# A gated attention block with a 32-expert layer: the gates are laid over the partitions by DMA, the output matrix is folded into the values, and all engines get new orders

## The chip, the cores and the metric

The kernel runs on one core of a Trainium2 chip. The metric is the device time of one execution in microseconds (us). Before the change it is 139.21 us, the median of three runs (139.1 to 139.27). The execution that the profiler recorded took 139.16 us; its span, from the first to the last recorded event, is 137.4 us, so 1.76 us lie around the span.

Engines are named as in the profile: PE is TensorE (PEld its weight loads), DVE is VectorE, ACT is ScalarE, POOL is GpSimd, SP is SyncE, which here only issues DMAs.

## The reference, cut to what matters

```python
# x (4, 256, 128), ctx (4, 256, 96), mask (4, 256) over ctx rows; 2 heads of 64; 32 experts of 64, top 4
xn = layernorm(ctx) * g + b;  ln = layernorm(layernorm(x)) * g + b
q  = ln @ Wq.T
kv = concat([xn @ Wkv.T, ln @ Wlkv.T], axis=1);  k, v = kv[..., :128], kv[..., 128:]
attn = softmax(where(mask, rmsnorm(q) * scale @ rmsnorm(k).T, -big))    # 256 queries x 512 keys, per head
x  = x + tanh(g_xattn) * ((attn @ v) @ Wo.T + bo)
xm = layernorm(x)
gates = sigmoid(xm @ expert_sel.T);  all but the 4 largest of 32 set to 0
h  = relu(einsum('nd,edf->nef', xm, keys)) * gates[:, :, None]
x  = x + tanh(g_ffn) * einsum('nef,efv->nv', h, values)
```

## The kernel before, in words

All data stays on the chip: 4 batches (b) of 256 rows, as 8 tiles of 128 rows. Each engine runs one list of stages, written out by hand in `PE_ORDER`, `DVE_ORDER` and `ACT_ORDER` (L56 to L99). A stage name stands in several lists, and semaphores tie its parts together. No scheduler moves anything: the list is the order.

Attention, per batch. `stats_in` and `norm_in` (DVE) normalize the rows, `turn_in` transposes them, and `project` (L746, L750) multiplies them by Wq and both key/value matrices in plain float32. ACT squares q and k and copies all of it from PSUM to `proj` (L603 to L611). `sum_qk` and `norm_qk` make the RMS norm, `turn_qk` transposes q and k and splits each into two float32r parts (`hi` and the rest `lo`), which PE multiplies faster than float32. `row_max` (PE L773, DVE L453) finds the largest score of each row, `turn_max` turns it into a row, and `weights b.i` (L801 to L807) computes scores minus maximum with the keys on the partitions, which ACT exponentiates into `prob` (L647). `attend b.a` (L818) multiplies by the values of head a, ACT copies the result to `oT` (L656), and `out_proj` (L828) applies Wo. DVE divides by the row sums and adds x (L468 to L478).

Expert layer. `stats_mid`, `norm_mid` and `turn_mid` make `xm`, transposed and split; `select` computes the gates on DVE; POOL cuts them into three bf16 parts (L342 to L345), and `turn_gates` transposes these. The expert columns are cut into 16 chunks of 128 (two experts each), the rows into two halves of 512. `up h.c` computes a chunk of hidden values in three float32r matmuls (L717 to L719) and spreads the gates of its two experts over the 128 partitions with a fourth matmul against a 0/1 matrix `expand` (L873). ACT applies the relu (L686), DVE multiplies by the spread gates (L542), ACT and DVE split the product into `hid_hi` and `hid_lo` (L693, L550), and `down h.c` adds three more matmuls into the accumulator of the half. `finish` turns the sum back with PE transposes (L892), and DVE adds the residual (L557).

Each engine waits in its own list: `up` on PE for the relu of two chunks before, `down` for both parts of its chunk. SP issues all input loads first (L277 to L286) and then waits for the results (L290).

## Time and profile before

| | |
|---|---|
| median of three runs | 139.21 us |
| profiled execution, its span | 139.16 us, 137.4 us |
| PE busy | 117.6 us, 86% |
| DVE busy | 108.7 us, 79% |
| ACT busy | 82.4 us, 60% |
| POOL busy | 18.6 us, 14% |
| largest DVE group (L542, gates times relu) | 32 x 689 ns |
| largest ACT groups (L693 split, L686 relu) | 32 x 628 ns, 32 x 596 ns |
| data moved by DMA | 4.28 MB, nearly all in the first 14 us |

Busy time of PE is the union of its records; the records of pipelined matmuls overlap, so the step from one start to the next is what a matmul costs in a row, and the mean duration is longer. A float32 matmul leaves two records, a float32r one leaves one. "Idle before" is the time that an engine stood still ahead of a group, with what ended it. Some matmul records are missing.

### The profile page before, as it was taken

What the parts mean: (1) busy time and instruction counts of PE and PEld (TensorE: products, weight loads), DVE (VectorE), ACT (ScalarE), POOL (GpSimd) and SP (SyncE); (2) the same over time, 40 slices, a digit from 0 to 9 for tenths busy, and PEclk for the clock granted to TensorE, in tenths of its full rate; (3) what the DMA queues carried; (4) which work ended last, traced back from release to release, by engine and by line L of the source; (5) the groups of instructions that cost most, each with busy time, mean ns of one, the idle gap of its engine ahead of it and who ended that gap; (6) DMA issues with size and microseconds to landing.
All of it is one profiled execution on the core that took longest, in us unless ns stands there. A gap on an engine that the chain in (4) does not pass through costs nothing.

```text
span 137.4 us, 2089 instructions
## 1 busy us (share of the span) xinstructions
PE 117.6 (86%) x616; PEld 81.3 (59%) x616; DVE 108.7 (79%) x333; ACT 82.4 (60%) x188; POOL 18.6 (14%) x43
## 2 busy tenths in 40 slices
PE   5917955696879799799896999999998999999990
PEld 5904534353646497378673676667766667767760
DVE  5877699887979959698496699998994799769852
ACT  5214698749893255337546756764575687587720
POOL 4050000700012493000330000004040000000000
PEclk9995599959999999999999999999999999999998
DMA  4699000000000000000000000000000000000004
GB/s 87 203 366 389 12 2 0 0 2 0 5 0 0 0 0 5 2 0 0 0 5 0 0 0 0 0 2 0 0 0 7 0 0 0 0 0 0 2 5 153
DMA packets 2171, 4.28 MB, mean 31 GB/s; under 512 B 240, under 2 KB 1648, under 8 KB 1904
## 3 DMA queue, kind: packets, MB, share of 16 engines
...
## 4 chain that ended last, share of the span: by engine, by line
PE 65%; DVE 18%; ACT 6%; issue 6%; POOL 1%; POOLq 1%; DVEq 0%; ACTq 0%
PE bank L717 10%; PE bank L719 9%; PE bank L718 9%; PE bank L818 9%; PE bank L873 5%; PE bank L746 4%; PE bank L750 3%; PE bank L828 3%; PE bank L773 3%; PE bank L801 2%; DVE keys L542 2%; PE bank L803 2%; PE bank L807 1%; PE bank L805 1%; DVE shift_l L365 1%
## 5 line engine op out<-in xcount | busy, mean ns | idle before, releaser
L542 DVE TENSOR_TENSOR keys<-bank,values 128x512 f32<-128x512 f32 x32 | 21.9, 689 | 7.6 <-ACT values L686 6.4
L686 ACT ACTIVATE values<-bank 128x512 f32<-128x512 f32 x32 | 19.1, 596 | 12.8 <-PE bank L719 12.8
L550 DVE TENSOR_TENSOR hid_lo<-keys,hid_hi 128x512 fp32r<-128x512 f32 x32 | 21.2, 683 | 0.8 <-ACT hid_hi L693 0.4
L693 ACT ACTIVATE hid_hi<-keys 128x512 fp32r<-128x512 f32 x32 | 19.6, 628 | 2.5 <-PE bank L719 1.6
L717 PE MATMUL bank<-hid_hi,v_lo 128*128 128x512 f32 x32 | 16.2, 506 | 0.0
L818 PE MATMUL bank<-prob,proj 128*65 128x256 f32 x64 | 15.1, 382 | 0.2 <-ACT prob L647 0.2
L717 PE MATMUL bank<-xm_hi,k_lo 128*128 128x512 f32 x32 | 14.6, 455 | 0.6 <-ACT gateT L677 0.6
L647 ACT ACTIVATE prob<-bank 128x512 f32<-128x512 f32 x16 | 8.9, 594 | 9.4 <-PE bank L807 7.8
L873 PE MATMUL bank<-gateT,expand 96*128 96x512 bf16 x32 | 12.5, 391 | 0.9 <-DVE keys L542 0.8
L719 PE MATMUL bank<-hid_hi,v_hi 128*128 128x512 f32 x32 | 12.7, 396 | 0.0
L718 PE MATMUL bank<-xm_lo,k_hi 128*128 128x512 f32 x32 | 12.6, 395 | 0.0
L718 PE MATMUL bank<-hid_lo,v_hi 128*128 128x512 f32 x32 | 12.6, 394 | 0.0
L719 PE MATMUL bank<-xm_hi,k_hi 128*128 128x512 f32 x32 | 12.6, 393 | 0.0
L453 DVE CUSTOM_DVE_ANT_0 junk<-bank,mask_b 128x512 bf16<-128x512 f32 x16 | 10.4, 689 | 2.5 <-PE bank L773 2.5
L818 PEld LDWEIGHTS bank<-prob,proj 128*65 128x65 f32 x64 | 8.4, 138 | 4.8 <-ACT prob L647 0.5
L746 PE MATMUL bank<-wa,xnT 128*128 128x384 f32 x16 | 8.8, 688 | 2.7 <-ACT xnT L591 2.7
L773 PE MATMUL bank<-kT_hi,qT_hi 64*128 64x512 f32 x16 | 6.3, 495 | 5.4 <-DVE mx L453 2.9
L325 POOL TENSOR_TENSOR k_lo<-keys,k_hi 128x512 fp32r<-128x512 f32 x4 | 5.0, 1269 | 32.5 <-ACT k_hi L621 32.5
L873 PEld LDWEIGHTS bank<-gateT,expand 96*128 96x128 bf16 x32 | 3.1, 96 | 10.5 <-DVE keys L542 5.8
L773 PEld LDWEIGHTS bank<-kT_hi,qT_hi 64*128 64x128 f32 x16 | 2.4, 183 | 9.2 <-DVE mx L453 5.9
L717 PEld LDWEIGHTS bank<-xm_hi,k_lo 128*128 128x128 f32 x32 | 6.1, 191 | 1.6 <-issue 0.7
L342 POOL CAST gate_p<-gate 128x64 bf16<-128x64 f32 x4 | 0.9, 237 | 44.4 <-DVE gate L531 44.4
...
## 6 DMA issues: line engine op xcount, KB each, us to landing
...
out<-x_mid SPq DMA_DIRECT2D x4, 128.0 KB, 1.9
...
cx<-ctx_in SPq DMA_DIRECT2D x2, 96.0 KB, 2.8
...
```

Source lines behind the costliest of these rows:

```text
L453: dve.tensor_tensor_reduce(junk[:, n % 2, :], bank_of(b, ROW_MAX + i)[:, :], mask_b[:, b, :], 1.0, SENTINEL, ALU.add, ALU.max, mx[:, b, i ...
L542: dve.tensor_tensor(hid[:, n % 3, :], gates_bank(n)[:, :], relu[:, n % 2, :], ALU.mult).then_inc(hid_ready, 1)
L550: dve.tensor_tensor(hid_lo[:, n % RING, :], hid[:, n % 3, :], hid_hi[:, n % RING, :].bitcast(F32), ALU.subtract).then_inc(hid_lo_ready, 1)
L686: act.activation(relu[:, n % 2, :], bank[H_BANK[n % 2]][:, :], ACT.Relu).then_inc(relu_ready, 1)
L693: act.activation(hid_hi[:, n % RING, :], hid[:, n % 3, :], ACT.Copy).then_inc(hid_hi_ready, 1)
L717: pe.matmul(o, ll, rh, start=start, stop=False)
L718: pe.matmul(o, lh, rl, start=False, stop=False)
L719: return pe.matmul(o, lh, rh, start=False, stop=stop)
L746: last = pe.matmul(bk[:, 0:G * DH], xnT[:, b, P * i:P * i + P], wa[:, A_LAT:A_LAT + G * DH], start=True, stop=True)
L773: pe.matmul(bank_of(b, ROW_MAX + i)[:, :], qT_hi[rows, b, P * t:P * t + P], kT_hi[rows, b, :], start=True, stop=True).then_inc(max_done, 1)
L818: last = pe.matmul(head_bank(b, a)[0:DH + 1, 0:S], proj[:, b, t, 4 + a, :], prob[:, a, t, :], start=(t == 0), stop=(t == KT - 1))
L873: pe.matmul(gates_bank(n)[:, :], expand[:, cc], half(gateT, h), start=True, stop=True).then_inc(spread_done, 1)
```

## The change

1. Gates. The `expand` matmul, POOL's three-part split and ACT's relu go. The gates are transposed in float32 (`turn_gates`), written by SP to a DRAM tensor `gate_rows`, and read back per chunk as a 128 x 512 tile `gated` (256 KB) in a ring of 6 slots: 64 copies outermost, the two experts inside. The columns of keys and values are interleaved to match. DVE's `up` takes relu and gate in one instruction, straight from PSUM.
2. The first 8 chunks of the first half (`WHOLE`) are not split; `down` multiplies them in plain float32, in one matmul each. The hidden banks become three.
3. Values. `fold` multiplies Wo into the value matrices once; `vlat` and `vctx` compute values that already carry Wo, one set of 128 columns per head. `project` keeps only q and k; `norm_qk` reads them from PSUM. `attend b.t` uses `prob` as the stationary side and gives rows by 129 columns, so `oT` and `out_proj` on PE go.
4. End. The output leaves transposed; `turn_res` transposes the residual ahead, and `finish` is one DVE instruction per batch.
5. Start. Most memsets leave DVE for POOL or become ACT copies; the 12 warm-up matmuls become 24 (`warm`), 16 of them ahead of `turn_in 0`. POOL makes the low parts of keys and values only behind the first matmul of each `row_max`.
6. All three order lists are new.

```diff
-WARM_UP = 12
+WARM_UP = 1
+WHOLE = 8
 # SP
-            sp.dma_start(wb[:, :], wb_in).then_inc(in_wb, 16)          # (now ahead of mask_in)
+            for h in range(HALF):
+                for b in range(HB * h, HB * h + HB):
+                    sp.wait_ge(gateT_ready, b + 1)
+                    sp.dma_start(gate_rows[:, S * b:S * b + S], gateT[:, b, :]).then_inc(rows_out[h], 16)
+                sp.wait_ge(rows_out[h], 16 * HB)
+                for c in range(EC):
+                    n = EC * h + c
...
+                    if n >= SLOTS:
+                        sp.wait_ge(hid_ready, n - SLOTS + 1)
+                    sp.dma_start(gated[:, n % SLOTS, :],
+                                 gate_rows[2 * c:2 * c + 2, HN * h:HN * (h + 1)].unsqueeze(0).to_broadcast([F, 2, HN])).then_inc(gated_in[n % SLOTS], 16)
 # DVE, up
-                dve.wait_ge(relu_ready, n + 1)
-                dve.wait_ge(spread_done, n + 1)
-                dve.tensor_tensor(hid[:, n % 3, :], gates_bank(n)[:, :], relu[:, n % 2, :], ALU.mult).then_inc(hid_ready, 1)
+                dve.wait_ge(up_done, n + 1)
+                dve.wait_ge(gated_in[n % SLOTS], 16 * (n // SLOTS + 1))
+                free_hid(n - 3)
+                dve.scalar_tensor_tensor(hid[:, n % 3, :], bank[H_BANK[n % len(H_BANK)]][:, :], 0.0, gated[:, n % SLOTS, :],
+                                         ALU.max, ALU.mult).then_inc(hid_ready, 1)
 # DVE, norm_qk
+                for lo, hi, src in ((0, KT * HEADS, bank_of(b, PROJECT)[:, :]), (KT * HEADS, NR, bank_of(b, PROJECT + 1)[:, 0:S])):
+                    dve.tensor_tensor(qk[:, b, lo:hi, :], src.rearrange("p (r d) -> p r d", d=DH),
...
 # ACT
+            def constants(i):
+                act.activation(ident_b[:, :], ident[:, :], ACT.Copy).then_inc(ident_b_ready, 1)
+                act.activation(mask_b[:, :, S:], ident[:, 0:1].unsqueeze(2).to_broadcast([P, B, S]), ACT.Copy,
+                               scale=0.0).then_inc(open_ready, 1)
+                act.activation(cnT[DC:DC + 1, :, :], ...
-                act.activation(relu[:, n % 2, :], bank[H_BANK[n % 2]][:, :], ACT.Relu).then_inc(relu_ready, 1)
-                act.activation(oT[:, b % 2, a, :], head_bank(b, a)[0:DH + 1, 0:S], ACT.Copy).then_inc(oT_ready, 1)
+                act.activation(vw[:, b, BT:, :, 0:D], value_bank(b, 0)[:, :]...   # vlat; vctx likewise
 # PE
+            def fold(i):
+                pe.wait_ge(wo_ready, 1)
+                for a in range(HEADS):
+                    pe.matmul(bank[7][:, D * a:D * a + D], wb[:, B_LV + D * a:B_LV + D * a + D], wo, start=True, stop=True)
...
+            def vlat(b):
+                        last = pe.matmul(o, lat, folded[:, D * a:D * a + D], start=True, stop=(a > 0))
+                        if a == 0:
+                            pe.matmul(o, wb[:, B_ONE:B_ONE + P], wb[:, B_WO:B_WO + D], start=False, stop=True)
+            def vctx(b):
+                    last = pe.matmul(bk[:, HEADS * D * t:HEADS * D * (t + 1)], cnT[:, b, P * t:P * t + P],
+                                     folded[0:DC + 1, HEADS * D:], start=True, stop=True)
-                    last = pe.matmul(head_bank(b, a)[0:DH + 1, 0:S], proj[:, b, t, 4 + a, :], prob[:, a, t, :],
+                        last = pe.matmul(bank_of(b, OUT + t)[:, WOA * a:WOA * a + WOA], prob[:, b % 2, a, j, P * t:P * t + P],
+                                         vw[:, b, j, a, :], start=(j == 0), stop=(j == KT - 1))
 # PE, down
+                if n < WHOLE:
+                    last = pe.matmul(bank[ACC_BANK[h]][:, :], values[:, cc], hid[:, n % 3, :],
+                                     start=(c == 0), stop=(c == EC - 1))
 # PE, up
-                pe.matmul(gates_bank(n)[:, :], expand[:, cc], half(gateT, h), start=True, stop=True).then_inc(spread_done, 1)
```

What the change moves shows at three places. First DVE's list from its start, before:

```order
L365 MEMSET shift_l 97x2048
L368 MEMSET shift_l 1x4x128 x2
L369 MEMSET mask_b 128x4x128
L370 MEMSET eps 128x1
L371 MEMSET shift_c 128x776
L373 MEMSET shift_c 128x8x2
L391 BN_STATS bn_in<-vecs_x 128x6 x2
```

and now:

```order
L360 MEMSET shift_l 97x2048
L379 BN_STATS bn_in<-vecs_x 128x6 [waits in_x0,dve_step]
L379 BN_STATS bn_in<-vecs_x 128x6
L382 BN_STATS bn_in<-cx 128x6 [waits in_cx0]
L382 BN_STATS bn_in<-cx 128x6
```

Five memsets and the small one behind them no longer stand ahead of the first statistics (`bn_in`). Second, PE's list where the attention ends and the expert layer begins (L855 turns gates, L818 attends, L717 to L719 and L873 are `up`, L836 turns `xm`, L828 is the output projection), before:

```order
L828 MATMUL bank<-wb,oT 128x129 x4
L855 MATMUL bank<-ident_b,gate_p 96x128 x2
L818 MATMUL bank<-prob,proj 65x256 x4
L855 MATMUL bank<-ident_b,gate_p 96x128 x2
L717 MATMUL bank<-xm_hi,k_lo 128x512
L718 MATMUL bank<-xm_lo,k_hi 128x512
L719 MATMUL bank<-xm_hi,k_hi 128x512
L873 MATMUL bank<-gateT,expand 128x512
```

and now (L879 turns gates, L854 attends, L705 to L707 are `up`, L862 turns `xm`):

```order
L879 MATMUL bank<-ident,gate 32x128 x2
L854 MATMUL bank<-vw,prob 128x129 x8
L879 MATMUL bank<-ident,gate 32x128 x2
L854 MATMUL bank<-vw,prob 128x129 x16
L705 MATMUL bank<-xm_hi,k_lo 128x512
L706 MATMUL bank<-xm_lo,k_hi 128x512
L707 MATMUL bank<-xm_hi,k_hi 128x512
L862 MATMUL bank<-ident,xn 128x128 x2
```

Both halves of the last batch's `attend` now stand between the second turned gates and the first chunk; before, one head of it and the last output projection followed inside the expert layer. Third, SP's queue behind the input loads, before:

```order
L286 DMA values<-values_in 128x2048
L290 DMA out<-x_mid 128x256 x4
```

and now (`inT` is the memory in which the ring `gated` lies):

```order
L288 DMA values<-values_in 128x2048
L292 DMA gate_rows<-gateT 32x256 [waits gateT_ready] x2
L302 DMA inT<-gate_rows 128x1x512 [waits vlat_done,vctx_done,proj_done,rows_out0]
L302 DMA inT<-gate_rows 128x1x512 x5
L302 DMA inT<-gate_rows 128x1x512 [waits hid_ready] x10
L292 DMA gate_rows<-gateT 32x256 [waits gateT_ready] x2
L302 DMA inT<-gate_rows 128x1x512 [waits hid_ready,rows_out1]
L302 DMA inT<-gate_rows 128x1x512 [waits hid_ready] x15
L306 DMA out<-x_mid0 128x256 [waits res_ready] x4
```

Four writes and 32 loads of 256 KB are added to a queue that had nothing to do there, and each load behind the sixth waits for DVE's product of six chunks before.

## Rows read from the trace of the kernel before

**Rows 1.** Four stretches of the span: busy us of each engine, clock, DMA.
```profile
0.00:35.25 35.25, 24.52 (x84) 16.15 (x85) 28.04 (x109) 21.18 (x62) 5.77 (x21) 0.85 0.30 103
35.25:72.92 37.67, 33.43 (x266) 23.67 (x265) 29.88 (x113) 20.82 (x47) 9.64 (x14) 1.00 0.01 2
72.92:132.48 59.56, 58.30 (x261) 40.70 (x261) 49.13 (x108) 39.77 (x78) 3.20 (x8) 1.00 0.00 1
132.48:137.40 4.92, 1.31 (x9) 0.76 (x7) 1.66 (x4) 0.66 (x2) 0.00 (x0) 0.88 0.34 110
```

**Rows 2.** Groups by shape: busy us, mean ns, idle before, releaser.
```profile
L542 DVE TENSOR_TENSOR keys<-bank,values 128x512 f32<-128x512 f32 x32 | 21.9, 689 | 7.6 <-ACT values L686 6.4 <-PE bank L873 0.6
L550 DVE TENSOR_TENSOR hid_lo<-keys,hid_hi 128x512 fp32r<-128x512 f32 x32 | 21.2, 683 | 0.8 <-ACT hid_hi L693 0.4 <-DVE keys L542 0.2 <-issue 0.2
L439 DVE SCALAR_TENSOR_TENSOR kT_lo<-bank,vecs_x,kT_hi 128x512 fp32r<-128x512 f32 x4 | 3.0, 738 | 0.5 <-ACT kT_hi L638 0.5
```

**Rows 3.** Timeline of PE, the last `down`: start, us, engine, line, operation.
```profile
132.02 0.39 PE L718 MATMUL bank<-hid_lo,v_hi 128*128 128x512 f32 x1
132.25 0.39 PE L719 MATMUL bank<-hid_hi,v_hi 128*128 128x512 f32 x1
```

**Rows 4.** Timeline of the front, DVE, ACT and PE, to the first row maximum.
```profile
1.24 1.76 DVE L365 MEMSET shift_l<- 97x2048 bf16 x1 [1.24 <-PEq L947]
2.94 0.20 ACT L583 ACTIVATE tanh_g<-vecs_x 128x2 f32<-128x2 f32 x1 [0.92 <-DMA vecs_x<-x_in]
...
6.02 0.28 DVE L391 BATCH_NORM_STATS2 bn_in<-vecs_x 128x6 f32<-128x128 f32 x1
...
11.11 0.56 ACT L591 ACTIVATE xnT<-bank,vecs_x 128x256 f32<-128x256 f32 x1 [3.33 <-PE bank L733]
...
16.89 0.95 DVE L423 TENSOR_REDUCE ss<-sq 128x12 f32<-128x768 f32 x1 [1.25 <-ACT sq L609]
...
24.40 0.80 PE L773 MATMUL bank<-kT_hi,qT_hi 64*128 64x512 f32 x2 [1.97 <-DVE kT_lo L439]
```

**Rows 5.** Stretches of the front by clock, same columns as Rows 1.
```profile
1.53:6.84 5.31, 5.31 (x24) 5.12 (x24) 4.61 (x14) 1.98 (x3) 0.68 (x8) 1.00 0.71 186
10.00:16.50 6.50, 5.75 (x14) 3.30 (x15) 4.75 (x30) 3.00 (x11) 0.21 (x1) 0.50 0.55 232
...
27.00:30.25 3.25, 3.25 (x7) 1.68 (x7) 3.11 (x12) 1.46 (x6) 0.00 (x0) 0.50 0.01 3
```

**Rows 6.** Timeline of PE: projection, attend and output projection at the full clock.
```profile
32.34 1.56 PE L746 MATMUL bank<-wa,xnT 128*128 128x384 f32 x4 [0.85 <-ACT xnT L591]
43.62 1.89 PE L818 MATMUL bank<-prob,proj 128*65 128x256 f32 x8
...
58.49 1.16 PE L828 MATMUL bank<-wb,oT 65*128 65x129 f32 x8
```

**Rows 7.** DMA: two stretches during the loads (columns as Rows 1).
```profile
3.75:5.00 1.25, 1.25 (x8) 1.25 (x7) 0.98 (x3) 0.69 (x1) 0.00 (x0) 1.00 0.90 331
5.00:6.50 1.50, 1.50 (x9) 1.50 (x9) 1.37 (x6) 0.00 (x0) 0.00 (x0) 1.00 0.47 108
```

**Rows 8.** DMA issues: KB each, us from issue to landing.
```profile
out<-x_mid SPq DMA_DIRECT2D x4, 128.0 KB, 1.9
cx<-ctx_in SPq DMA_DIRECT2D x2, 96.0 KB, 2.8
```

**Rows 9.** Timeline of PE: the first chunk of the expert layer.
```profile
72.92 0.47 PE L717 MATMUL bank<-xm_hi,k_lo 128*128 128x512 f32 x1 [0.56 <-ACT gateT L677]
```

**Rows 10.** Timeline of the end, PE, ACT, DVE, SP's queue.
```profile
132.48 1.35 PE L892 MATMUL bank<-ident,xn 128*128 128x128 f32 x8
132.68 0.66 ACT L699 ACTIVATE xn<-bank 128x256 f32<-128x256 f32 x2 [1.89 <-PE bank L719]
133.12 1.66 DVE L557 SCALAR_TENSOR_TENSOR x_mid<-bank,tanh_g,x_mid 128x256 f32<-128x256 f32 x4 [1.55 <-PE bank L892]
133.63 1.80 SPq L290 DMA_DIRECT2D out<-x_mid  x4
```

More of the change, by code:

```diff
@@ L41 @@
 HN = HT * P
-G = 6
+SLOTS = 6
 NR = KT * HEADS + BT * HEADS
@@ L56 @@
 PE_ORDER = """
-    turn_in 0, project 0, turn_in 1, project 1, turn_in 2, turn_qk 0, row_max 0, project 2, turn_max 0,
-    turn_in 3, project 3, weights 0.0, turn_qk 1, weights 0.1, turn_qk 2, row_max 1, attend 0.0, turn_max 1,
-    attend 0.1, row_max 2, weights 1.0, turn_qk 3, out_proj 0, turn_max 2, weights 1.1, weights 2.0, attend 1.0,
-    attend 1.1, row_max 3, out_proj 1, weights 2.1, turn_max 3, turn_mid 0, attend 2.0, select 0, weights 3.0,
-    turn_mid 1, attend 2.1, select 1, weights 3.1, out_proj 2, turn_gates 0, attend 3.0, turn_gates 1, up 0.0,
@@ new lines @@
+    row_max 0, vlat 2, vctx 2, turn_max 0, project 2, turn_in 3, weights 0.0, vlat 3, turn_qk 1, vctx 3,
+    project 3, turn_qk 2, weights 0.1, row_max 1, attend 0.0, turn_max 1, attend 0.1, weights 1.0, row_max 2,
+    weights 1.1, turn_qk 3, turn_max 2, attend 1.0, row_max 3, attend 1.1, turn_max 3, weights 2.0, turn_mid 0,
+    weights 2.1, weights 3.0, turn_mid 1, select 0, attend 2.0, select 1, weights 3.1, turn_gates 0, attend 2.1,
+    turn_gates 1, attend 3.0, attend 3.1, up 0.0, turn_mid 2, up 0.1, select 2, up 0.2, up 0.3, down 0.0, up 0.4,
@@ L69 @@
+    turn_res 2, up 1.13, up 1.14, up 1.15, down 1.9, down 1.10, down 1.11, down 1.12, down 1.13, down 1.14,
+    down 1.15, turn_res 3
 """
 DVE_ORDER = """
[L71 to L74 removed]
@@ new lines @@
+    norm_qk 2, turn_qk 1, row_max 1, sum_qk 3, turn_qk 2, turn_max 1, norm_qk 3, row_max 2, out_proj 0,
+    turn_max 2, stats_mid 0, turn_qk 3, row_max 3, norm_mid 0, out_proj 1, stats_mid 1, turn_max 3, turn_mid 0,
+    norm_mid 1, turn_mid 1, select 0, select 1, out_proj 2, stats_mid 2, norm_mid 2, out_proj 3, turn_mid 2,
+    up 0.0, up 0.1, up 0.2, stats_mid 3, up 0.3, norm_mid 3, up 0.4, select 2, turn_mid 3, up 0.5, up 0.6,
+    select 3, up 0.7, up 0.8, up 0.9, split 0.8, up 0.10, up 0.11, split 0.9, split 0.10, up 0.12, up 0.13,
@@ new lines @@
+    turn_in 2, stats_in 3, vctx 1, split_keys 2, split_keys 3, vlat 2, sum_qk 1, vctx 2, project 2, turn_in 3,
+    weights 0.0, sum_qk 2, vlat 3, split_values 2, vctx 3, split_values 3, turn_qk 1, turn_qk 2, project 3,
+    weights 0.1, sum_qk 3, weights 1.0, weights 1.1, turn_qk 3, stats_mid 0, weights 2.0, turn_mid 0,
+    stats_mid 1, weights 2.1, turn_mid 1, weights 3.0, select 0, select 1, weights 3.1, turn_gates 0,
+    turn_gates 1, stats_mid 2, turn_mid 2, stats_mid 3, select 2, turn_mid 3, select 3, split 0.8, split 0.9,
@@ L897, in _ @@
+            run = {"warm": warm, "turn_in": turn_in, "project": project, "turn_qk": turn_qk, "row_max": row_max, "turn_max": turn_max,
+                   "weights": lambda at: weights(*at), "fold": fold, "vlat": vlat, "vctx": vctx, "attend": lambda at: attend(*at),
                    "turn_mid": turn_mid, "select": select, "turn_gates": turn_gates,
-                   "up": lambda at: up(*at), "down": lambda at: down(*at), "finish": finish}
+                   "up": lambda at: up(*at), "down": lambda at: down(*at), "turn_res": turn_res}
```

524 lines of the change are left out of this document (262 added, 262 removed).

## The prediction, made before the changed kernel had run

> **What bounds the kernel now.** I cut the span where the work changes its kind and read the busy time of each engine in the four stretches [rows 1]. From 72.92 to 132.48 us, the expert layer, PE is busy 58.30 of 59.56 us, DVE 49.13, ACT 39.77: PE sets the time. From 35.25 (first `weights`) to 72.92 PE is busy 33.43 of 37.67. Before 35.25 nobody is full: PE 24.52, DVE 28.04, ACT 21.18 of 35.25. There a chain runs from DVE to PE to ACT and back, and PE runs part of it at half clock: the granted clock is 0.50 from 10.0 to 16.5 and again from 27.0 to 30.25, the level of 1.2 GHz [rows 5]. The warm-up ahead of it steps by 5.31/24 = 0.22 us, where L828's float32 records of nearly the same width take at most 1.16/8 = 0.145 [rows 6]; whatever its clock column says (1.00), it ran slowly too. The last stretch is a tail of 4.92 us. So I price PE's list in stretches two and three, the chain in the first, and the tail.
>
> **Expert layer, the sure part.** In a row a float32r matmul of 512 columns steps by 0.23 us [rows 3]. Before, 32 chunks took 32 x 7 = 224 of them, 52.1 us at 0.2325. In the same 59.56 us lay one head of `attend` (8 records, 1.75) and one output projection (0.95), both from [rows 6]. These 54.8 go. In come `up`, 96 x 0.2325 = 22.3; `down` of the 24 split chunks, 72 x 0.2325 = 16.7; `down` whole, 8 float32 matmuls of 512 columns; and four `turn_res`, 8 transposes at 0.13 = 1.0 (L892's eight, less the drain [rows 10]). L818's float32 records of 256 columns step by 0.216 (1.89 less one duration of 0.38, over 7 [rows 6]); a matmul leaves two, so 512 columns cost 4 x 0.216 = 0.87, and 8 of them 7.0, 1.4 more than 8 split ones. In: 47.0. So 59.56 - 54.8 + 47.0 = 51.8; all else in the stretch, its 1.3 us of PE idle time too, stays.
>
> Does another engine take over? ACT loses its 32 relus, so no. DVE has two 512-column instructions per split chunk: 689 + 683 = 1.37 us by L542 and L550, or 738 + 683 = 1.42 if the new product costs what L439 does, the nearest three-operand instruction from PSUM [rows 2]. PE's six matmuls are 1.40. At worst 24 x 0.02 = 0.5; I take 0, since the durations of neighbours overlap a little. The selects and norms on DVE lie in the first 8 chunks, where DVE has one such instruction and 8 x 0.7 = 5.6 us of room more.
>
> **The gates' journey, the unsure part.** Before, gates turned on ACT were followed by the first matmul after 0.56 us of idle time [rows 9]. Now: ACT copy 0.4, SP writes (32 KB, priced as a 128 KB store, 1.9 [rows 8]), SP waits, loads 256 KB. No row shows a load of that size alone; 96 KB landed in 2.8 among others [rows 8], so I take 2.6 and keep 2 and 4 as ends. Together about 5.2 us from the second `turn_gates` to the first product. Behind that `turn_gates` PE has `attend` 3.0 and 3.1 (32 records, 3.9) and three `up` (9 x 0.2325 = 2.1) before it needs a product: 6.0 us, and a `turn_mid` and a `select` besides. This is the cover; without it the cost is the whole 5.2. The second half repeats it: the writes wait behind ACT's 11th split, and I find the first load landing about when DVE wants it, 0 to 1 us late.
>
> Then 32 loads must keep up with 1.40 us per chunk, that is 187 GB/s; six slots give 8 us of lead. The loads of the inputs ran at 331 GB/s at their best before 5 us, which makes 0.8 us per chunk [rows 7]. But from 5.0 to 6.5 us, when by the bytes moved so far the mask load was on the queue, only 108 GB/s moved and the DMA engines were 0.47 busy [rows 7]. The mask load is the one broadcast in the trace: one row of 1 KB read 128 times. At 108 GB/s a chunk takes 2.43. I take a middle value below 1.40, because the new load reads two rows of 2 KB side by side and six can be in flight, and keep 2.43 as the bad end.
>
> The Trainium skill, "DMA: Bandwidth & Descriptors", section "Why a DMA increments its semaphore by 16 and not by 1", says that a DMA spreads over as many engines, at most 16, as divide the slowest dimension of both sides. With 64 copies outermost against 128 partitions that is 16; with the two rows outermost it would be 2. No run here shows it yet; by it the load is not confined, and my sum stands.
>
> **Attention, second stretch.** Before, 37.67 us from `weights` 0.0 to `up` 0.0. Seven heads of `attend` (7 x 1.75 = 12.3) and three output projections (2.9) go. In come all four batches of the new `attend`, 4 x 32 float32 records of 129 columns. Half of L818's step is 0.109, L828's full 0.145 [rows 6]: 14.0 to 18.6; I take 0.123, near the lower end because L828's figure holds its drain: 15.8. Also new here are `project` 3, `vlat` 3 and `vctx` 3, which were or would be part of the front: 4 records of 256 columns and 4 of 128 (1.3), 12 of 128 (1.3), 4 of 256 (0.9). So 37.67 - 15.2 + 15.8 + 3.5 = 41.8 (40.0 to 44.6).
>
> **The front.** I follow the chain against [rows 4]. x has landed at 2.94 and DVE's remaining memset ends at 3.0, so the statistics start 3 us earlier than 6.02. The context lands about 4.0 and ACT's second table load ends 4.44; normalized rows are there at 7.3 instead of 10.3. ACT puts three constant copies (0.3 + 1.0 + 1.0, from 594 ns for 512 columns) in between, so the first turned rows leave ACT from 9.3 instead of 11.11. PE then has `fold` (8 records, 0.9) and q and k of batch 0 (1.3), at full clock if the longer warm-up holds it: squares by 12.1, sum at 12.3 instead of 16.89. Here ACT loses part again: `vlat`, two splits and `project` 1 stand ahead of the root that `norm_qk` 0 needs, DVE idles near 2 us, and `row_max` 0 starts at 22.3 instead of 24.40. `weights` 0.0 needs `row_max` (3.5), `norm_in` 3, `turn_max` and the mask rows (now 2 x 0.4 to 0.8): 29.5 instead of 35.25. Most of this 5.75 is order, since `project` 3 is paid for later, above.
>
> Two edits I cost at nothing. POOL makes the low parts of keys and values only behind each `row_max` (keys by the second, near 40 us; `up` 0.0 wants them at 71), and POOL is busy 18.6 of 137.4 us. The input loads total 110 KB less to wa and 70 KB more to wb, which now stands ahead of the mask: x and context of batches 2 and 3 are wanted near 11 us and land about 10. If they are late, it is by tenths, in a chain that has slack of 2 us behind it on DVE.
>
> **Tail.** From the end of the last matmul (132.5) to DVE's last result 2.3, then 2.6 to the end [rows 10]. Now DVE reads the accumulator directly, but `turn_res` 3 stands behind the last `down`: 0.3 PE, 0.45 ACT, 0.5 DVE, so 1.3 and 2.6.
>
> **Sum.** 29.5 + 41.8 + 51.8 + 3.9 = 127.0 of span against 137.4. With the 1.76 around the span 128.8, against 139.16 of the profiled run and 139.21 of the median, which agree.
>
> **The rivals.** (A) *The stream of gates is the bound, slower than before.* For it: the 108 GB/s of the only broadcast; 32 loads where none were, on a queue that waits in order. Against it: the larger pieces and the cover. At 2.43 us each from 70.3 us on (`up` 0.0 at 71.3, less 3.8 of `attend`, plus 2.8 for copy, write and issue), the last lands at 148.1; product 0.7, the two splits 1.3, `down` 0.7 and the tail 3.9 add 6.6: 154.7 + 1.8 = 156.5. It turns the sign above 1.89 us per load (139 GB/s), where (137.4 - 6.6 - 70.3)/32 lies; from 1.57 us on it eats 0.32 us of the gain per 0.01. In sentences of their own: the Trainium skill, same page, section "Anatomy of one DMA", gives a fixed 2.0 us plus bytes over 436 GB/s, 2.6 us for one such load. If loads did not overlap, 32 would take 83 us and the time would be about 162. The trace does not agree: the four stores, 1.9 us each [rows 8], are all issued and done in the 3.8 us from 133.63 to the end of the span [rows 10], half of what they would take one by one.
> (B) *The gains of the front do not carry.* DVE and ACT queues hold each other, the clock falls again, `attend` steps at 0.136, DVE's product at 0.74 makes the split chunks DVE-bound (24 x 0.1). `up` 0.0 then at 74, 54 us of expert layer and 3.9 of tail: 131.9 + 1.8 = 133.7, in a spread of 132 to 136. For it: the first stretch has no full engine, so order alone decides, and I could follow it only once.
> (C) *Waits vanish.* The list without relu and spread couples PE to one engine only. PE idled 4.2 us in the second stretch and 1.3 in the third [rows 1]; with 3 of these gone and `attend` at 0.109 (1.8): 124.0.
>
> **How the numbers follow.** Forecast (126 to 131.5) 0.50, B 0.22, C 0.15, A 0.13. A and the worst of B lie outside the range on one side, half of C's tail on the other: 124 to 136. What a measurement here can tell from no change is about 0.2%, 0.3 us; A below its threshold counts as faster. Faster 0.87, same 0.01, slower 0.12.
>
> **What would show it.** In the profile after: `up` 0.0 on PE near 71.3; PE busy nearly all through the expert layer, with about 225 records in it where 261 were; DVE's products waiting for PE, not for DMA; loads of 256 KB landing within 3 us. `weights` 0.0 near 29.5 and a granted clock of 1.00 from 10 to 30 us. I am wrong if DVE idles for `gated<-gate_rows` by more than a few us, or if PE's clock is 0.50 in the front.

## The result, and the profile after

The changed kernel takes 124.58 us (median of four runs, 122.81 to 125.02) against 139.24 us of the kernel before on the same chip: ratio 0.8881, 95% interval 0.874 to 0.902. The forecast of 128.8 had the sign and most of the size, but was 4.2 us too slow. Its range began at 124.0: the median lies just inside, the 123.7 that the ratio gives just below. The profiled run took 122.81 us, span 120.7, mean granted clock 0.998. Four of 14 runs of this kernel had such a clock (122.8 to 123.0 us); in the others one stretch or more ran at half clock (0.986: about 124.4; 0.973: 127.0). The ten later ones stood beside the experiments, with medians of 125.16 and 124.36. Below, a time at a lower clock is compared with these at like mean clock, or with the 122.8 where the half clock lies right behind a wait that the edit makes.

The stretches of [rows 1], cut at the same events: first `weights`, first `up`, and what follows the last `down`. Behind them the two clock stretches of [rows 5] and one of the gates' loads (columns as there).

```profile
0.00:27.62 27.62, 25.05 (x157) 22.36 (x158) 23.27 (x95) 20.44 (x46) 5.44 (x18) 1.00 0.39 131
27.62:67.35 39.73, 36.24 (x337) 31.30 (x337) 32.55 (x124) 19.22 (x47) 7.50 (x6) 1.00 0.01 3
67.35:117.27 49.92, 49.25 (x214) 37.03 (x213) 44.18 (x99) 18.21 (x35) 0.00 (x0) 1.00 0.54 170
117.27:120.70 3.43, 0.38 (x3) 0.14 (x1) 0.97 (x2) 0.38 (x1) 0.00 (x0) 0.95 0.46 153
72.00:76.00 4.00, 4.00 (x14) 2.27 (x13) 3.64 (x13) 0.50 (x2) 0.00 (x0) 1.00 0.97 307
10.00:16.50 6.50, 6.50 (x50) 6.16 (x49) 6.22 (x33) 4.72 (x13) 0.00 (x0) 1.00 0.56 237
27.00:30.25 3.25, 3.23 (x36) 2.80 (x35) 3.08 (x8) 2.72 (x6) 0.00 (x0) 1.00 0.00 0
```

| | before | forecast | after |
|---|---|---|---|
| to `weights` 0.0 | 35.25 | 29.5 | 27.62 |
| to `up` 0.0 | 37.67 | 41.8 | 39.73 |
| expert layer | 59.56 | 51.8 | 49.92 |
| tail | 4.92 | 3.9 | 3.43 |

PE is busy 49.25 of 49.92 us in the expert layer, and its granted clock is 1.00 in the two stretches of the front where it was 0.50. The loads of gates run at 307 GB/s with the DMA engines 0.97 busy: 256 KB in 0.85 us, not the 2.43 of the bad end. The groups that answer to [rows 2], and the loads (KB each, us to landing):

```profile
L528 DVE SCALAR_TENSOR_TENSOR keys<-bank,inT 128x512 f32<-128x512 f32 x32 | 21.2, 684 | 3.2 <-PE bank L707 1.2 <-DMA inT<-gate_rows 0.9 <-PE bank L908 0.7
L545 DVE TENSOR_TENSOR hid_lo<-keys,hid_hi 128x512 fp32r<-128x512 f32 x24 | 16.0, 685 | 1.1 <-ACT hid_hi L682 1.0
...
L854 PE MATMUL bank<-vw,prob 128*128 128x129 f32 x128 | 15.8, 278 | 0.2 <-ACT prob L651 0.2
...
inT<-gate_rows SPq DMA_DIRECT2D x32, 256.0 KB, 3.6
```

The merged product costs 684 ns, like the plain one (689), and DVE waited for the loads 0.9 us in all. A load lands 3.6 us after its issue (median), later than the 2.6 of the forecast and the 3 that it named as a sign. The timeline of the front (against [rows 4]), of the gates' journey, of `attend` and whole `down` (L908), and of the end:

```profile
3.08 0.49 DVE L379 BATCH_NORM_STATS2 bn_in<-vecs_x 128x6 f32<-128x128 f32 x2
...
8.80 0.55 ACT L596 ACTIVATE inT<-bank,vecs_x 128x256 f32<-128x256 f32 x1
...
12.39 0.94 DVE L411 TENSOR_REDUCE ss<-sq 128x12 f32<-128x768 f32 x1
...
17.38 0.17 DVE L354 SCALAR_TENSOR_TENSOR rs_qk<-rs_qk 128x12 f32<-128x12 f32 x1 [0.87 <-ACT rs_qk L574]
...
20.74 1.04 PE L808 MATMUL bank<-kT_hi,qT_hi 64*128 64x512 f32 x2
...
63.64 0.38 PE L879 MATMUL bank<-ident,gate 128*32 128x128 f32 x2
...
63.85 3.74 PE L854 MATMUL bank<-vw,prob 128*128 128x129 f32 x32
...
64.05 0.37 ACT L674 ACTIVATE gateT<-bank 32x256 f32<-32x256 f32 x1 [1.00 <-PE bank L879]
...
66.78 3.81 SPq L302 DMA_DIRECT2D inT<-gate_rows  x6
...
69.81 0.69 DVE L528 SCALAR_TENSOR_TENSOR keys<-bank,inT 128x512 f32<-128x512 f32 x1
...
77.61 1.88 PE L908 MATMUL bank<-keys,values 128*128 128x512 f32 x4
...
117.03 0.40 PE L707 MATMUL bank<-hid_hi,v_hi 128*128 128x512 f32 x1
117.27 0.38 PE L929 MATMUL bank<-ident,x_mid 128*128 128x128 f32 x2
117.53 1.05 DVE L552 SCALAR_TENSOR_TENSOR x_mid<-bank,tanh_g,xn 128x256 f32<-128x256 f32 x2 [0.61 <-PE bank L707]
```

`attend` steps by (3.74 - 0.28)/31 = 0.112 us, whole `down` by 0.43 a record ((1.88 - 0.59)/3), 0.86 a matmul, as priced. From the second turned gates to the first product it is 6.2 us (5.2 forecast), and when that product starts DVE has just finished other work, without a wait.

### The profile page after: what moved, and what is told of

It reads as the page before. It is cut to its first block, busy times and chain, and to the rows that moved or that the text cites. A ratio compares the mean times of both kernels' runs of the same rounds, so it can differ in the third digit from the quotient of the medians.

```text
span 120.7 us, 2176 instructions
## 1 busy us (share of the span) xinstructions
PE 110.9 (92%) x704; PEld 90.8 (75%) x704; DVE 101.0 (84%) x319; ACT 58.3 (48%) x128; POOL 12.9 (11%) x24
## 4 chain that ended last, share of the span: by engine, by line
PE 81%; DVE 7%; ACT 5%; issue 4%; POOL 0%; DVEq 0%; POOLq 0%
PE bank L705 11%; PE bank L707 11%; PE bank L706 11%; PE bank L854 10%; PE bank L714 7%; PE bank L908 6%; PE bank L781 3%; PE bank L808 3%; PE bank L767 3%; PE bank L835 2%; PE bank L735 2%; ACT prob L651 2%; PE bank L841 2%; PE bank L837 2%; PE bank L839 1%
## 5 line engine op out<-in xcount | busy, mean ns | idle before, releaser
L528 DVE SCALAR_TENSOR_TENSOR keys<-bank,inT 128x512 f32<-128x512 f32 x32 | 21.2, 684 | 3.2 <-PE bank L707 1.2
L545 DVE TENSOR_TENSOR hid_lo<-keys,hid_hi 128x512 fp32r<-128x512 f32 x24 | 16.0, 685 | 1.1 <-ACT hid_hi L682 1.0
L854 PE MATMUL bank<-vw,prob 128*128 128x129 f32 x128 | 15.8, 278 | 0.2 <-ACT prob L651 0.2
L854 PEld LDWEIGHTS bank<-vw,prob 128*128 128x128 f32 x128 | 14.8, 191 | 0.9 <-issue 0.8
L705 PE MATMUL bank<-xm_hi,k_lo 128*128 128x512 f32 x32 | 14.8, 462 | 0.0
L707 PE MATMUL bank<-xm_hi,k_hi 128*128 128x512 f32 x32 | 12.6, 395 | 0.0
L714 PE MATMUL bank<-ident 128*128 128x128 f32 x48 | 9.5, 364 | 1.5 <-POOL ident L314 1.5
L714 PEld LDWEIGHTS bank<-ident 128*128 128x128 f32 x48 | 8.9, 276 | 1.6 <-POOL ident L314 1.5
L705 PE MATMUL bank<-hid_hi,v_lo 128*128 128x512 f32 x24 | 9.6, 399 | 0.0
L707 PE MATMUL bank<-hid_hi,v_hi 128*128 128x512 f32 x24 | 9.5, 396 | 0.0
L908 PE MATMUL bank<-keys,values 128*128 128x512 f32 x16 | 7.8, 592 | 0.0
L706 PEld LDWEIGHTS bank<-xm_lo,k_hi 128*128 128x128 f32 x32 | 6.0, 189 | 1.9 <-issue 1.0
L705 PEld LDWEIGHTS bank<-xm_hi,k_lo 128*128 128x128 f32 x32 | 6.0, 188 | 2.0 <-issue 1.0
L707 PEld LDWEIGHTS bank<-xm_hi,k_hi 128*128 128x128 f32 x32 | 6.0, 188 | 1.5
```

The lines of the kernel that those rows point to most:

```text
L528: dve.scalar_tensor_tensor(hid[:, n % 3, :], bank[H_BANK[n % len(H_BANK)]][:, :], 0.0, gated[:, n % SLOTS, :], ALU.max, ALU.mult).then_inc ...
L545: dve.tensor_tensor(hid_lo[:, m % RING, :], hid[:, n % 3, :], hid_hi[:, m % RING, :].bitcast(F32), ALU.subtract).then_inc(hid_lo_ready, 1)
L705: pe.matmul(o, ll, rh, start=start, stop=False)
L706: pe.matmul(o, lh, rl, start=False, stop=False)
L707: return pe.matmul(o, lh, rh, start=False, stop=stop)
L714: pe.matmul(bank[5][:, 0:P], ident[:, :], ident[:, :], start=True, stop=True)
```

## The experiments

My theory of the missing 4 us: PE is the bound throughout. Before, waits were hidden inside its busy time, in the loop of spread, relu and product, and went away with that loop; in the front the warm-ups held the clock. The rival: DVE, the lists' order or the stream of gates hold part of the time, and no single edit carries the gain.

### What sets the expert layer

One more matmul per chunk on PE, with nothing waiting for it:

```diff
+                pe.matmul(bank[H_BANK[n % 3]][:, :], k_hi[:, cc], half(xm_hi, h), start=True, stop=True)
                 product(bank[H_BANK[n % 3]][:, :], (k_hi[:, cc], k_lo[:, cc]), ...
```

> The changed kernel with one more float32r matmul of 512 columns ahead of each chunk's three, into the same bank, its result overwritten; nothing waits for it. Theory (PE is full in the expert layer): 32 x 0.23 = 7.4 us slower than the changed kernel, less the 0.7 us of PE idle time there, 6.7 to 7.4. Rival (DVE, at 1.37 us a chunk against PE's 1.40, or the loads of gates at 0.85, already hold part of it): under 5 slower. The difference between the kernel with spread and relu and this one is the price of the waits alone.

Median 130.35. At the full clock it is 129.5 us against 122.8: 6.7 more, for 7.4 us of matmuls. PE is the bound of the changed kernel; DVE at 0.88 of the stretch is not.

The spread and the relu put back. The edit is larger than the lines shown: the gates no longer go through DRAM and are single bf16 values, there are two hidden banks instead of three, and the lists of PE and ACT are changed around them.

```diff
+                pe.matmul(gates_bank(n)[:, :], expand[:, cc], half(gateT, h), start=True, stop=True)
+                act.activation(relu[:, n % 2, :], bank[H_BANK[n % 2]][:, :], ACT.Relu)
-                dve.scalar_tensor_tensor(hid..., bank[...], 0.0, gated[:, n % SLOTS, :], ALU.max, ALU.mult)
+                dve.tensor_tensor(hid..., gates_bank(n)[:, :], relu[:, n % 2, :], ALU.mult)
```

> The changed kernel with the gates spread by a PE matmul per chunk again, the relu back on ACT, two hidden banks, no gates through DRAM (the gates are one bf16 value each instead of three parts, so their low bits are left out). Theory (PE sets the time, and before the change the chain PE, relu, product, spread hid waits inside PE's busy time): 32 x 0.23 = 7.4 us for the matmuls plus 1.4 to 3 of waits, 9 to 10.5 us slower than the changed kernel. Rival 1 (only the matmuls count, the waits came from elsewhere): 7.4 slower. Rival 2 (the expert layer is not bound by PE; the gain is in the front): under 3 slower.

151.63 us (150.1 at a mean clock of 0.974), 26.5 more than the 125.16 of the unaltered kernel beside it. The half clock of its profile lies in the first quarter of the expert layer (0.56 and 0.58 from 72 to 80 us), behind 4 us in which PE was busy 2.17, so I count it to the edit. Against the 129.5 of the kernel with one more matmul per chunk, 20.6 us are waits and the clock that fell behind them, not 1.4 to 3. DVE's product there (line number of that kernel) waits mostly for the relu:

```profile
L521 DVE TENSOR_TENSOR keys<-bank,inT 128x512 f32<-128x512 f32 x32 | 22.0, 688 | 22.7 <-ACT inT L673 13.6
```

The old loop with fewer banks, in a list written for the new one, is far worse than in its own list, so this does not price the waits of the kernel before. Those I took from the other side, in the old kernel. First the spread alone goes (but for two chunks), then the relu as well. Both leave out the gates of nearly all chunks, as does the third below, so only their time is of use:

```diff
-                pe.matmul(gates_bank(n)[:, :], expand[:, cc], half(gateT, h), start=True, stop=True)   # only n = 0 (and 17) stay
-                act.activation(relu[:, n % 2, :], bank[H_BANK[n % 2]][:, :], ACT.Relu)                 # second kernel; one tile of gates
+                dve.scalar_tensor_tensor(hid..., bank[H_BANK[n % 2]][:, :], 0.0, relu[:, 0, :], ALU.max, ALU.mult)
```

> The kernel before with the matmul that spreads the gates run for chunk 0 and chunk 17 alone; the other 30 chunks are multiplied by what stands in those two banks, so their gates are left out. ACT's relu and everything else stay. Theory (each such matmul costs PE 0.23 us and its wait for DVE's product of the chunk before costs more): 30 x 0.2325 = 7.0 us plus part of the 1.4 us of hidden waits and 1.3 of idle time: 7.0 to 9 faster than before, 130 to 132. Rival (ACT with relu and split, or DVE, takes over at once): 3 to 5 faster.

> As the one before, and also ACT's relu merged into DVE's product, with one tile of gates, spread once and copied once, for all chunks (the gates of the other chunks are left out): the inner loop of the changed kernel in the old order, without any load of gates. Theory (the relu on ACT between PE and DVE was the second part of the hidden waits): 31 x 0.2325 = 7.2 us plus 1.4 + 1.3: 8.5 to 10 faster than before, 129 to 130.5, and 1 to 2 faster than the one that keeps the relu. Rival (the relu on ACT hides under PE wholly): within 0.3 us of the one that keeps it.

The first: ratio 0.9634 (0.956 to 0.970), 133.7 to 134.1 at 0.958, where the kernel before took 138.2 to 139.2 beside it: 5 us faster, not 7 to 9. The second: 0.967 (0.962 to 0.972), and 0.9609 (0.954 to 0.968) when run again; 134.1 to 134.5 at 0.961 (seven of the first ten runs had 0.913 to 0.932, and 137.5 to 138.7 us). Taking the relu off ACT brought nothing more. Its expert layer:

```profile
72.80:127.40 54.60, 51.42 (x231) 39.59 (x232) 48.29 (x108) 24.18 (x47) 3.20 (x8) 1.00 0.00 1
```

PE lost 7.2 us of work and the stretch 4.96: PE now idles 3.2 us where it idled 1.3. Of the 3.2, it waits 2.2 for DVE (product 1.5, `xm_lo` 0.7) and 1.0 for POOL's gates. Before, PE's tally is 54.8 by the prediction's prices and 2.1 us, my estimate, for `turn_mid`, `select` and `turn_gates`: 56.9. Its busy time is 58.3, so 1.4 us of waits lay unseen inside it. Here the tally is 56.9 - 7.2 = 49.7 and the busy time 51.4: 1.7 us lie unseen. These hidden waits were not those of relu and spread; the tallies are good to about 0.5 us.

Does DVE hold it? The same kernel with the first 8 chunks whole:

```diff
+                if n < WHOLE:                       # 8
+                    pe.matmul(bank[ACC_BANK[h]][:, :], values[:, cc], hid[:, n % 3, :], ...)
-    up 0.8, turn_mid 3, up 0.9, select 2, down 0.4, up 0.10, down 0.5, down 0.6, up 0.11
+    up 0.8, down 0.4, turn_mid 3, up 0.9, down 0.5, down 0.6, select 2, up 0.10, up 0.11
```

> The kernel before without the spreading matmul and the relu on ACT once more, as the measure for the one beside it: 134.0 to 134.5 us at a mean clock of 0.961, 138 at 0.925.

> The kernel before in its own order, without the spreading matmul and ACT's relu as in the earlier run (gates of chunk 0 for all chunks), and now also with the first 8 chunks multiplied whole in float32: 8 splits each go from DVE and ACT; four down stages stand one or two places earlier on PE, since three hidden tiles force it. Theory (in the old order DVE, at 48.3 busy us of 54.6, took over from PE when the spread went, and kept 2.3 of its 7.2 us; the 8 splits are what gives DVE room): PE gains 1.4 us of work, DVE loses 5.5, and the expert layer falls from 54.6 to 51 to 53: 131.5 to 133 at the same clock, 1.5 to 3 faster than the kernel without whole chunks. Rival (PE's own list held the time, and whole chunks only cost PE): 1.4 us slower than it.

141.4 to 141.8 at 0.961 to 0.963, over 7 us slower than the 134.3 beside it. Neither the theory's 1.5 to 3 faster nor the rival's 1.4 slower comes out, and the run does not decide whether DVE held the time, since it brings a new wait of its own. The timeline of PE and of DVE:

```profile
84.32 0.50 PE L720 MATMUL bank<-xm_hi,k_lo 128*128 128x512 f32 x1 [0.89 <-DVE keys L545]
87.04 0.50 PE L720 MATMUL bank<-xm_hi,k_lo 128*128 128x512 f32 x1 [0.89 <-DVE keys L545]
...
86.29 0.69 DVE L545 SCALAR_TENSOR_TENSOR keys<-bank,sq 128x512 f32<-128x512 f32 x1 [1.35 <-PE bank L883]
```

A chunk takes 2.7 us there, though PE has 1.57 of work in it. PE's `up` waits for DVE's product of two chunks before (two hidden banks). That product waits for a whole `down` on PE (L883 there; the hidden tile is read until it ends). And that `down` stands in PE's list behind the `up` in between, so the three follow one another instead of overlapping. In the changed kernel, which has a third bank and a list with `down` three chunks behind `up`, whole chunks follow each other in 1.56 us (L908 starts at 72.02, 73.58 and 75.14); which of the two breaks the circle was not run apart.

Fewer whole chunks in the changed kernel, none and four (the latter with 12 warm-ups):

```diff
-WHOLE = 8
+WHOLE = 0        # and WHOLE = 4; the splits 0.0 (0.4) to 0.7 placed in DVE's and ACT's lists
```

> The changed kernel with all 32 chunks split in two parts as before (no chunk multiplied whole in float32). Theory (the 8 whole chunks cost PE 8 x 0.87 - 24 x 0.23 = 1.4 us and save DVE 8 x 0.68 = 5.5 in a stretch in which DVE was busy 44.2 of 49.9 us): DVE would be busy 49.7 of what PE could do in 48.5, so DVE sets the first half and the kernel is 1 to 3 us slower. Rival (only PE's tally counts): 1.4 us faster, 121.4 at the full clock.

> The changed kernel with 12 warm-ups in all (as in the run with 12) and 4 whole chunks instead of 8, the four splits put behind select 2 and select 3 on DVE. Theory (PE sets the time and DVE has 5.7 us of room in the expert layer): 4 x (0.87 - 0.70) = 0.7 us faster than with 8, 121.5 at the full clock. Rival (DVE's and ACT's lists couple there, as in the kernel without whole chunks, which came out 8 us slower): 1 to 5 us slower than 122.2.

None: 131.71, ratio 0.9418 (0.933 to 0.951); 130.7 and 131.1 at 0.970, some 8 us more than 122.8, not 1 to 3. (At like mean clock it would be 4, but the half clock of this profile lies in the expert layer right behind PE's waits, so it belongs to the price.) Four: 124.27, ratio 0.8958 (0.886 to 0.906), 124.0 to 125.4 at the full clock where the kernel with 8 and as many warm-ups has 121.7 to 122.6, so 2 more, not 0.7 less. PE's tally alone is refuted both times. Without whole chunks PE idles early in the layer, and then its clock falls:

```profile
76.00:80.00 4.00, 1.99 (x7) 0.97 (x6) 3.09 (x12) 1.13 (x3) 0.00 (x0) 1.00 0.38 123
80.00:82.00 2.00, 1.12 (x3) 0.92 (x4) 1.25 (x3) 0.63 (x1) 0.00 (x0) 0.62 0.04 15
```

DVE is not full there either (3.09 of 4.00 us). In that layer PE waits only for DVE (product 2.5 us, `xm_lo` 1.8, split 1.1), and DVE waits 4.6 us for ACT's part of the split. That points to the order in which I put the splits beside norms and selects; no better order was run, and how much one would recover stays open.

### The gates' journey

Three edits, one per block: `attend` ahead of the second turned gates; each load issued twice (the semaphores of the copy are not shown); the two rows outermost, with the columns of keys and values in plain order to match (not shown):

```diff
-    turn_gates 1, attend 3.0, attend 3.1, up 0.0
+    attend 3.0, attend 3.1, turn_gates 1, up 0.0
```
```diff
+                    sp.dma_start(spare[:, n % 4, :], gate_rows[2 * c:2 * c + 2, ...])     # same source, memory nobody reads
```
```diff
-   gate_rows[2 * c:2 * c + 2, ...].unsqueeze(0).to_broadcast([F, 2, HN])
+   gate_rows[2 * c:2 * c + 2, ...].unsqueeze(1).to_broadcast([2, F, HN])
```

> The changed kernel with both halves of the last batch's attend ahead of the second turned gates instead of behind them (PE's list alone; no instruction more or less). Theory (the gates' way through DRAM, 6.2 us from the second turned gates to the first product, is longer than what PE has left to do, and the attend covers it): 3.74 us of attend leave the cover, so 3 to 3.7 us slower at the same clock, 125.8 to 126.5 at the full clock, and DVE's first product waits that much longer for the load. Rival (nothing on PE is so near that wait; the three banks of hidden values absorb it): under 1 us slower.

127.46, ratio 0.9063 (0.898 to 0.915); 126.2 and 126.7 at 0.986, and none of the four runs at the full clock. The first products there, and the clock of the two stretches around and behind them:

```profile
72.90 1.38 DVE L528 SCALAR_TENSOR_TENSOR keys<-bank,inT 128x512 f32<-128x512 f32 x2 [1.43 <-DMA inT<-gate_rows]
74.68 0.69 DVE L528 SCALAR_TENSOR_TENSOR keys<-bank,inT 128x512 f32<-128x512 f32 x1 [0.41 <-DMA inT<-gate_rows]
```
```profile
72.00:76.00 4.00, 3.58 (x13) 2.31 (x12) 2.66 (x7) 0.00 (x0) 0.00 (x0) 0.75 1.00 306
76.00:80.00 4.00, 4.00 (x12) 2.24 (x10) 2.87 (x12) 0.75 (x3) 0.00 (x0) 0.82 0.80 269
```

`weights` 0.0 and `up` 0.0 start there at the same time as in the changed kernel (27.6 and 67.3), so nothing is lost before the edit. The first product starts at 72.90 instead of 69.81, 3.1 us later. The clock then falls right behind PE's waits, and the whole comes to 3.4 to 3.9 us more than 122.8. The cover is real, and the forecast of 3 to 3.7 held: nearly all of the 3.7 us were needed.

> The changed kernel with each load of gates issued a second time into memory that nothing reads: 512 KB per chunk instead of 256. A load took 0.85 us of a full DMA (307 GB/s at a busy share of 0.97), two take 1.7 us per chunk against PE's 1.40. Theory (the stream has slack now, 0.85 against 1.40, and becomes the bound when doubled): the last product can start about 66.8 + 32 x 1.7 + 1.5 = 122.7 instead of some 112, so 5 to 8 us slower. Rival 1 (the 307 GB/s were asked for and not the limit; the loads run faster when more are asked): within 1 us. Rival 2 (the stream is already the bound, with the waits spread thinly): 20 us or more slower, since 32 x 0.85 come on top.

136.33, ratio 0.9823 (0.976 to 0.989); 135.6 at 0.987, 12.8 more than 122.8. (The clock of that profile is 0.72 from 104 to 110 us, behind 4 us in which PE was busy 1.18, so it is counted in.) The rate and the turn between the halves:

```profile
72.00:76.00 4.00, 3.79 (x12) 1.89 (x11) 2.02 (x7) 0.12 (x1) 0.00 (x0) 1.00 0.96 326
110.00:116.00 6.00, 5.95 (x26) 4.48 (x25) 4.78 (x8) 2.40 (x4) 0.00 (x0) 1.00 0.99 286
```
```profile
96.99 0.68 DVE L553 TENSOR_TENSOR hid_lo<-keys,hid_hi 128x512 fp32r<-128x512 f32 x1
100.62 0.69 DVE L536 SCALAR_TENSOR_TENSOR keys<-bank,inT 128x512 f32<-128x512 f32 x1 [2.95 <-issue]
102.83 0.69 DVE L536 SCALAR_TENSOR_TENSOR keys<-bank,inT 128x512 f32<-128x512 f32 x1 [1.52 <-DMA inT<-gate_rows]
```

The DMA engines are full at 286 to 326 GB/s, so the stream has the slack of 0.85 against 1.40 us and no more: doubled, it is the bound. My 5 to 8 us left out that the second half's rows are written only after the first half's loads have been issued, which costs a full stream 3 to 4 us; DVE stands still for 2.95 and 1.52 us there.

> The changed kernel with the two experts' rows outermost and the 64 copies inside in each load of gates, and keys and values in their plain column order to match; the same bytes. Theory (what the trace of the changed kernel shows is a load over all DMA engines, busy share 0.97 at 307 GB/s, whatever the order of the copies, since 128 partitions are written either way): within 0.5 us. Rival: the load is cut along its outermost dimension, two pieces on two engines at an eighth of the rate, 8 x 0.85 = 6.8 us per load, 32 of them 218 us from 66.8 on: about 290 us. In a sentence of its own: by the Trainium skill, 'DMA: Bandwidth & Descriptors', section 'Why a DMA increments its semaphore by 16 and not by 1', the number of engines is the largest up to 16 that divides the slowest dimension of both sides, here 2, which is this rival.

248.13 us, ratio 1.774 (1.758 to 1.789). The same stretch of the loads:

```profile
72.00:76.00 4.00, 1.03 (x6) 0.55 (x5) 0.00 (x0) 0.00 (x0) 0.00 (x0) 0.94 0.13 51
```

The busy share is 0.13, about what two of 16 engines make (0.125), at 51 GB/s: 5.1 us per load instead of 0.85. Each of the two then moves 25.5 GB/s, where 16 together move 307, 19 each; hence 248 and not 290. The Trainium skill, "DMA: Bandwidth & Descriptors", section "Why a DMA increments its semaphore by 16 and not by 1", has the number of engines as the largest up to 16 that divides the slowest dimension of both sides, here 2; the trace agrees. Putting the copies outermost, with interleaved expert columns to allow it, is worth about 123 us here.

### The front

Three blocks: fewer warm-ups (12, all ahead of `turn_in 0`, and in another kernel one); the constants back on DVE; and, in the kernel before, more warm-ups (22 ahead instead of 12, and 19 between the stages).

```diff
-    warm 13, ..., turn_in 0, warm 16, fold 0, project 0, warm 17, warm 18, vctx 0, ...     # 12 warm-ups, none between
+    turn_in 0, fold 0, project 0, vctx 0, ...                                               # and, in another, one warm-up
```
```diff
+                then(dve.memset(shift_l[row:row + 1, :, S:], 0.0))      # constants on DVE again, ahead of the statistics:
+                dve.memset(mask_b...); dve.memset(eps...); dve.memset(shift_c...)
```
```diff
-    turn_in 0, project 0, turn_in 1, project 1, ...                     # kernel before
+    turn_in 0, warm 4, project 0, warm 1, turn_in 1, warm 4, project 1, ...
```

> The changed kernel with only 12 of its 24 warm-up matmuls, all ahead of the first transposes, none between the stages of the front. Theory (the front gained from the full granted clock between 10 and 30 us, which the warm-ups hold): the granted clock falls to 0.50 for a stretch of 3 to 6.5 us in the front, as before the change, and weights 0.0 starts at 29 to 31 instead of 27.62: 1.5 to 3 us slower than the changed kernel. Rival (the new order alone fills PE enough, or PE is not what the front waits for): within 0.5 us of 122.8.

> The changed kernel with 12 warm-ups in all, once more with more runs. Theory (fewer fillers on PE make the stretch at half clock rarer, and spare weights 0.0 half a microsecond): median 122.2 to 122.6, most runs at a mean clock of 0.998 or above, 1 to 2% faster than the changed kernel by the medians. Rival (the first four runs were luck): 0.5 us faster at the same clock, and half clock in as many runs as the changed kernel beside it.

> The changed kernel again beside the three others: 122.8 us where the mean granted clock is 1.00, some 2 us more where one stretch at half clock lies in it. In its first eight runs that was so in six.

> The changed kernel with one warm-up matmul instead of 24. Theory (the order of the front fills PE well enough by itself; what the first warm-ups do is to raise the clock before the first transposes): the front runs at half clock for a stretch of a few us and comes out 1 to 3 us later, 123.5 to 125.5. Rival (even the first are useless): within 0.3 us of the kernel with 12.

Twelve warm-ups: 122.4, ratio 0.8771 (0.869 to 0.885), and 123.62, 0.8803 (0.872 to 0.888), beside 124.36, 0.8921 (0.884 to 0.900) of the changed kernel. At the full clock 121.7 to 122.6 against 122.8 to 123.0. One: 124.7, 0.8943 (0.887 to 0.902), 123.5 to 125.1 in the four runs whose clock column says 1.00. So as long as the clock holds, the fillers between the stages do nothing for the front, and the first twelve are worth about 2 us. The version with twelve beats both kernels by the medians, but the intervals overlap, and three of its ten runs had a clock of 0.947 to 0.959 (126.9 to 129.9), lower than any of the changed kernel's 14. Whether the fillers guard against that is not settled. In one profile with twelve the clock stays at 1.00 though PE works less than half of the first stretch:

```profile
7.00:10.00 3.00, 1.43 (x11) 1.18 (x11) 2.60 (x16) 1.57 (x5) 0.12 (x1) 1.00 1.00 334
10.00:16.50 6.50, 6.50 (x50) 6.09 (x48) 6.22 (x31) 5.29 (x14) 0.92 (x1) 1.00 0.59 247
```

In the profile of one of those three (129.9 us) it does not. There `weights` 0.0 starts at 33.9 us instead of 27.1, with a clock in the front nearly as low as before the change:

```profile
7.00:10.00 3.00, 0.74 (x4) 0.42 (x4) 2.83 (x16) 1.78 (x5) 1.04 (x1) 0.82 0.91 317
10.00:16.50 6.50, 6.50 (x27) 5.73 (x28) 4.18 (x21) 1.69 (x6) 0.00 (x0) 0.56 0.58 245
27.00:30.25 3.25, 3.25 (x15) 3.07 (x15) 2.03 (x10) 1.69 (x4) 0.00 (x0) 0.50 0.03 5
```

What the first twelve do shows in the projection of batch 0, first in the changed kernel, then with one warm-up (profiled run, 128.7 us). The same four records take 1.91 us instead of 1.03, and all of PE's records step at half speed up to 15.6 us. The clock column says 1.00 there, as it does over the warm-ups in [rows 5], so it cannot be read that early:

```profile
9.71 1.03 PE L735 MATMUL bank<-wa,inT 128*128 128x256 f32 x4
11.40 1.91 PE L735 MATMUL bank<-wa,inT 128*128 128x256 f32 x4
```

> The changed kernel with its constant tiles made by DVE ahead of its first statistics, as before the change, instead of by POOL and ACT. Theory (the start of the statistics, 3.08 against 6.02 before, passes through the chain of the front to weights 0.0): statistics 2.5 to 3 us later, weights 0.0 2 to 3 us later than 27.62, 2 to 3 us slower. Rival (the chain has slack behind the statistics, the wait on ACT and on the context load hides it): under 1 us slower.

128.83, ratio 0.9245 (0.917 to 0.932); 127.4 to 127.5 at 0.986, 3.0 more than the changed kernel. The statistics start at 5.84 instead of 3.08, and `weights` 0.0 at 31.95 instead of the 29.2 of an unaltered profile with the same clock: the whole delay passes through.

```profile
5.84 0.27 DVE L381 BATCH_NORM_STATS2 bn_in<-vecs_x 128x6 f32<-128x128 f32 x1
```

> The kernel before, with 22 warm-up matmuls instead of 12 and 19 more put between the stages of its front; nothing else. Theory (the half clock at 10.0 to 16.5 and 27.0 to 30.25 costs the chain of the front): the granted clock is 1.00 there, PE's 9.0 busy us of those stretches shrink to some 5, of which half lies on the chain: weights 0.0 at 33 instead of 35.25, 2 us faster than before (1 to 4). Rival (the clock in the front is a sign of an idle PE and costs little; the 12 warm-ups of the changed kernel did as well as 24): within 0.5 us of before.

137.57, ratio 0.9889 (0.980 to 0.998); `weights` 0.0 at 33.5 instead of 35.25, 1.7 earlier, with the clock still short of full from 10 to 16.5:

```profile
10.00:13.00 3.00, 2.96 (x15) 2.10 (x16) 2.25 (x16) 1.43 (x4) 0.13 (x1) 0.76 0.98 415
13.00:16.50 3.50, 3.50 (x17) 2.54 (x16) 2.87 (x16) 2.51 (x9) 0.00 (x0) 0.72 0.07 28
```

## Why the prediction missed, point by point

**Where it held.** PE bounds the expert layer (one more matmul per chunk: 6.7 of 7.4 us). The work in the expert layer was priced rightly: float32r steps 0.23, whole `down` 0.86. The product cost 0.684, its lower price. The load of gates takes neither 2.43 us nor a turn of its own, and the cover counts (without it the first product starts 3.1 us later). The 2.6 us that the prediction cites for one such load from the Trainium skill, "DMA: Bandwidth & Descriptors", section "Anatomy of one DMA", is that page's fit for DMAs issued from POOL; these are issued by SP, and landed after 3.6. The 3 us by which the statistics start earlier pass through whole (constants back on DVE: 3.0).

**The step that failed** is "So 59.56 - 54.8 + 47.0 = 51.8; all else in the stretch, its 1.3 us of PE idle time too, stays", and with it the same assumption for the second stretch. A stretch minus a tally is not a constant. Before, 59.56 less the tally of 56.9 left 2.7 us of waits. After, 49.92 less 49.1 (22.3 + 16.7 + 7.0 + 1.0, and the 2.1) leaves 0.8. That is the 1.9 by which this stretch was too long. It was rival C, at 0.15, that had it, and I priced C's idle time from the busy column alone, which shows 1.3 of the 2.7: records of 0.39 us that step by 0.23 can hide waits of up to 0.16 between them. Which edit took these waits away is not shown. Removing spread and relu in the old list left them (1.7), so my explanation by that coupling, made after the result, fell too. The two parts that I tried alone, spread with relu and whole chunks, were worth 5 us and less than nothing in the old list; with the third bank and the new list the layer lost 9.6.

**Second stretch**, 2.1 too long, and below its own range of 40.0 to 44.6. Here the larger part is a price: `attend` at 0.123 where 0.112 is measured, 128 x 0.011 = 1.4 us. The lower end, half of L818's step [rows 6], was right, and the 0.145 of L828 should have had no weight since it held its drain. The other 0.7 is idle time, 3.5 instead of 4.2, carried over again. What folding Wo into the values is worth by itself was not run.

**Front**, 1.9 too long: turned rows 0.5 early, the sum of squares as forecast, then `norm_qk` 0 with 0.87 us of wait where I had "near 2", so `row_max` 0 at 20.74 instead of 22.3; the rest of the chain ran as priced. The twelve added warm-ups have no part in it: with 12 in all, and the clock held, `weights` 0.0 stood at 27.1. **Tail**, 0.5 too long: `finish` of batch 2 runs while ACT copies the residual of batch 3. The four terms, 1.9, 2.1, 1.9 and 0.5, all erred to the same side: 1.4 us by the price of `attend`, nearly all of the rest by waiting times that I carried over or put in.

**Against the median.** The stretches miss by 6.3 us, the median by 4.2. Of the difference, 0.3 lies around the span (2.1 instead of 1.76), and 1.8 is the clock: 10 of 14 runs had half clock somewhere, which a forecast from one profile did not hold. That the median came within 4.2 is luck to that extent.
